# Two cross-attention blocks on one core: layer 1 keys and values from one column-tiled product, keys copied through DRAM, strided 32x32 transposes, all orders rewritten

## The reference

```python
# layer 0
qn, kn, vn = ln(x), ln(ctx), ln(ctx)
p = softmax((qh @ kh.T + rel_bias[idx]) / 8)            # 16 heads, 128 x 128 each
x = x + (p @ vh) @ fc_w.T + fc_b
x = x + gelu(ln2(x) @ W1.T + b1) @ W2.T + b2
# layer 1
q = x @ Wq + bq                                         # 16 heads of 16
k = ctx @ Wk + bk;  v = ctx @ Wv + bv                   # one head of 16 each
attn = softmax(window(q @ k.T / 4)) @ v @ Wo + bo
gate = silu(concat(attn, x) @ Wg + bg)
out = attn * gate + x * (1 - gate)
y = out * rsqrt(mean(out * out) + 1e-6) * rms_w
return y - mean(y over tokens)
```

## Time and profile before

| what | value |
|---|---|
| runs | 1901.46, 1903.86, 1906.15 us, median 1903.86 |
| profiled execution: its own time, and its span from first to last instruction | on record only as the span, 1903.7 us on its one core |
| PE busy | 1840.5 us, 97% |
| PEld, DVE, ACT, POOL busy | 89%, 80%, 81%, 68% |
| the chain that ended last | PE 94%, DMA 2%, DVE 1%, ACT 1%, POOL 1%, issue 1% |
| DMA | 214.49 MB, 113 GB/s mean |

### The profile page before, as it was taken

How to read it: one execution, slowest core, us unless ns; L and a number is a source line. 1 busy time by engine, 2 the same in 40 slices (tenths; PEclk the granted TensorE clock), 3 DMA queues, 4 the chain that set the end, 5 groups by cost and what they waited for, 6 DMA issues and landing times.

```text
span 1903.7 us, 55010 instructions
## 1 busy us (share of the span) xinstructions
PE 1840.5 (97%) x18660; PEld 1696.0 (89%) x18660; DVE 1518.9 (80%) x6787; ACT 1538.4 (81%) x5586; POOL 1294.2 (68%) x1328
## 2 busy tenths in 40 slices
PE   5999999999999999999999999999999999999974
PEld 4899999999999999999999999999999999999963
DVE  6768888888888888888888888888888888878764
ACT  4688888888888888888888888888888888888864
POOL 3547776767776767777766777766777776777654
PEclk9999999999999999999999999999999999999997
DMA  6434444444444444454434454444444444444332
GB/s 208 131 84 116 111 119 111 115 110 115 107 118 120 115 107 114 104 123 121 116 99 121 101 125 118 114 102 118 111 118 118 110 107 113 112 116 114 88 83 56
DMA packets 215273, 214.49 MB, mean 113 GB/s; under 512 B 29904, under 2 KB 197456, under 8 KB 214992
## 3 DMA queue, kind: packets, MB, share of 16 engines
q1 hardware_dynamic: 214992, 210.97, 44.5%
HBM read 67.23 MB, written 9.44 MB: 40 GB/s over the span
## 4 chain that ended last, share of the span: by engine, by line
PE 94%; DMA 2%; DVE 1%; ACT 1%; POOL 1%; issue 1%; SPq 0%; ACTq 0%; DVEq 0%; POOLq 0%
PE bank L576 12%; PE bank L577 11%; PE bank L578 11%; PE bank L594 8%; PE bank L590 8%; PE bank L591 8%; PE bank L757 7%; PE bank L770 7%; PE bank L582 4%; PE bank L882 4%; PE bank L895 3%; PE bank L583 3%; PE bank L586 3%; PE bank L654 2%; PE bank L600 2%
## 5 line engine op out<-in xcount | busy, mean ns | idle before, releaser
L2574 ACT ACTIVATE soft<-soft,row_min 128x128 f32<-128x128 f32 x1024 | 397.4, 393 | 16.3 <-DVE row_min L1728 16.0
L2494 ACT ACTIVATE soft<-soft,row_min 128x128 f32<-128x128 f32 x1024 | 397.8, 394 | 9.5 <-DVE row_min L1620 9.1
L235 DVE STREAM_TRANSPOSE turned<-soft 128x512 f32<-128x512 f32 x512 | 349.2, 692 | 9.7 <-POOL soft L3032 4.9
L3032 POOL TENSOR_TENSOR soft<-soft,inv_sum 128x512 f32<-128x512 f32 x256 | 267.1, 1044 | 127.3 <-DVE inv_sum L1628 123.3
L3041 POOL TENSOR_TENSOR soft<-soft,inv_sum 128x512 f32<-128x512 f32 x256 | 264.9, 1045 | 93.0 <-DVE inv_sum L1737 93.0
L1620 DVE CUSTOM_DVE_ANT_0 soft<-bank,relb 128x128 f32<-128x128 f32 x1024 | 231.6, 284 | 64.9 <-PE bank L757 64.5
L1728 DVE CUSTOM_DVE_ANT_0 soft<-bank,winb 128x128 f32<-128x128 f32 x1024 | 226.6, 284 | 16.9 <-PE bank L882 14.5
L2494 ACT ACTIVATION_READ_ACCUMULATOR soft<-soft,row_min 128x1 f32 x1024 | 196.7, 192 | 0.0
L2574 ACT ACTIVATION_READ_ACCUMULATOR soft<-soft,row_min 128x1 f32 x1024 | 195.1, 191 | 0.0
L1691 DVE TENSOR_TENSOR hidS<-hid,hidS 128x1024 fp32r<-128x1024 f32 x64 | 120.5, 1883 | 71.5 <-ACT hidS L2545 68.6
L757 PE MATMUL bank<-kT,qT 64*128 64x128 f32 x2048 | 148.7, 285 | 1.5 <-DVE kT L1600 1.4
(11 more groups left out here) (255 smaller groups left out, 6538.3 us busy)
## 6 DMA issues: line engine op xcount, KB each, us to landing
soft<-turned SPq DMA_DIRECT2D x1024, 128.0 KB, 2.8
tokens<-stats_by_row SPq DMA_DIRECT2D x63, 256.0 KB, 3.3
tokens<-in_x SPq DMA_DIRECT2D x32, 256.0 KB, 3.1
raw<-in_x_t SPq DMA_DIRECT2D x32, 256.0 KB, 2.8
x<-in_x SPq DMA_DIRECT2D x32, 256.0 KB, 3.1
out<-gate SPq DMA_DIRECT2D x63, 128.0 KB, 3.1
tokens<-in_ctx SPq DMA_DIRECT2D x31, 256.0 KB, 2.8
raw<-in_ctx_t SPq DMA_DIRECT2D x31, 256.0 KB, 2.8
```

Source lines behind the costliest of these rows:

```text
L235: return eng.transpose(turned[:, slot, :, s % 2, :, :].rearrange("p j h b -> p h j b"), soft[:, s, :, :].rearrange("p h (j a) -> p h j a", ...
L2494: last = act.activation(soft[:, s, h, :], soft[:, s, h, :], ACT.Exp, bias=row_min[:, s, h:h + 1], scale=-1.0, accum_out=row_sum[:, s, h:h ...
L2574: last = act.activation(soft[:, s, h, :], soft[:, s, h, :], ACT.Exp, bias=row_min[:, s, h:h + 1], scale=-1.0, accum_out=row_sum[:, s, h:h ...
L3032: pool.tensor_tensor(soft[:, m % NS0, :, :], soft[:, m % NS0, :, :], inv_sum[:, m % NS0, :].unsqueeze(2).broadcast_to([P, QUAD, SEQ]), ALU ...
```

## The change

One product `kv` takes the place of `kv_k` and `kv_v`: `Wk` and `Wv` side by side (32 columns), in column quarters, in block order. It gives each quarter of a bank 16 rows of keys and 16 rows of values for 32 tokens of each batch. `kv_turn` adds the key bias while it copies the whole piece (128x64) to `key_rows`, and transposes the same piece to `by_key`; `kv_out` puts the values once into the middle of `vpad`. The keys go to DRAM by four DMAs (`keys_out`) and back by two (`keys_in`) to the even rows of `kpar[:, 0]` and the odd rows of `kpar[:, 1]`; the other rows are zeros written once. The columns of `Wq` of layer 1 are mixed in pairs to fit. The keys now stand in token order: `k_out` reads the bank without a step, and `turn_blocks` reads every fourth element of a row instead. The constants `block_of`, `pair_of` and `parity` go. `scores1` waits for `keys_in`, not `kv_out`. The rings of banks and the lists of all five engines are written anew.

```diff
-        wkv1 = sb("wkv1", [P, KD, P + 2 * HD])
+        wkv1 = sb("wkv1", [P, KD, 2 * HD])
...
         def turn_blocks(eng, slot, s):
             return eng.transpose(turned[:, slot, :, s % 2, :, :].rearrange("p j h b -> p h j b"),
-                                 soft[:, s, :, :].rearrange("p h (j a) -> p h j a", j=NB))
+                                 soft[:, s, :, :].rearrange("p h (a j) -> p h j a", j=NB))
...
+            def keys_out(g):
+                if not there(g):
+                    return
+                till.wait_ge("kv_turn", g + 1)
+                if g >= 1:
+                    till.wait_ge("keys_in", 32 * g)
+                for j in range(NB):
+                    sp.dma_start(t["key_rows"][:, :, j, :], key_rows[j * BLOCK:j * BLOCK + HD, :, :]).then_inc(
+                        sem["keys_out"], 16)
+
+            def keys_in(g):
...
+                    till.wait_ge("scores1", GROUP * g)
+                till.wait_ge("keys_out", 16 * NB * (g + 1))
+                rows_of = t["key_rows"].rearrange("e b j a -> e (b j a)").unsqueeze(0).broadcast_to([NT1, HD, TOK])
+                for i in range(2):
+                    sp.dma_start(kpar[i:P:2, i, :], rows_of).then_inc(sem["keys_in"], 16)
...
-                for k in range(KD):
-                    last = pe.matmul(bank[:, 0:TOK], wkv1[:, k, 0:P], src[:, k, :], start=(k == 0), stop=(k == KD - 1))
-                last.then_inc(sem["kv_k"], 1)
...
-                        last = pe.matmul(bank[j * BLOCK:(j + 1) * BLOCK, TOK:TOK + GROUP * BLOCK], wkv1[:, k, P:P + HP],
+                        last = pe.matmul(bank[j * BLOCK:(j + 1) * BLOCK, 0:GROUP * BLOCK], wkv1[:, k, :],
                                          of_block[:, j, :, :], start=(k == 0), stop=(k == KD - 1), skip_group_check=True)
-                last.then_inc(sem["kv_v"], 1)
+                last.then_inc(sem["kv"], 1)
...
-                for i in range(2):
-                    dve.tensor_scalar(kpar[:, i, :].rearrange("p (b j a) -> p b j a", b=GROUP, j=NB),
-                                      bank[:, 0:TOK].rearrange("p (b a j) -> p b j a", b=GROUP, j=NB), bk1[:, 0:1],
-                                      parity[:, i:i + 1], ALU.add, ALU.mult)
-                dve.transpose(v_twice[:].rearrange("p b e -> p (b e)"), bank[:, TOK:TOK + GROUP * BLOCK]).then_inc(
-                    sem["kv_turn"], 1)
+                of_bank = bank[:, 0:GROUP * BLOCK]
+                dve.tensor_scalar(key_rows[:].rearrange("p b a -> p (b a)"), of_bank, bk1[:, 0:1], None, ALU.add)
+                dve.transpose(by_key[:].rearrange("p b e -> p (b e)"), of_bank).then_inc(sem["kv_turn"], 1)
...
-                    last = dve.tensor_scalar(kT[:, c, :].rearrange("p (b j a) -> p b j a", b=GROUP, j=NB),
-                                             bank[:, c * TOK:(c + 1) * TOK].rearrange("p (b a j) -> p b j a", b=GROUP, j=NB),
-                                             bk[:, i:i + 1], None, ALU.add)
+                    last = dve.tensor_scalar(kT[:, c, :], bank[:, c * TOK:(c + 1) * TOK], bk[:, i:i + 1], None, ALU.add)
```

Of the rewritten order of DVE's prologue:

```diff
             moments_x(0)
+            var_x(0)
             stats_c(0)
             moments_c(0)
-            bias_out(bq, banks[5], 2, -SCALE0)
-            var_x(0)
+            flip_x(0)
+            var_c(0)
...
```

More of the change, by code:

```diff
@@ L19 @@
 PER_GROUP = dict(
-    turn_h=1, turn_x2=1, kv_k=1, kv_v=1, proj_q=4, proj_k=4, proj_v=4, scores=4, turn0=8, pv=4,
+    turn_h=1, turn_x2=1, kv=1, proj_q=4, proj_k=4, proj_v=4, scores=4, turn0=8, pv=4,
     fc=4, fc_lo=4, w1=4, w2=4, w2_lo=4, out_mm_lo=2, q1=1, scores1=2, turn1=8, pv1=4, out_mm=2, center=2,
@@ L640, in wo_wg, with kv @@
                 last.then_inc(sem["wo_wg"], 1)
-            def kv_k(g, bank, *drains):
+            def kv(g, bank, *drains):
                 if not there(g):
@@ new lines, in tensor_program @@
+            proj_q(0, 0, banks[7])
+            kv(0, banks[6])
+            bias_mm(banks[5], SOFT1, 1, shifts[2], 0)
+            bias_mm(banks[5], SOFT0, 2, shifts[2], 1)
+            proj_q_lo(0, banks[7])
+            proj_k(0, 0, banks[0], ("bias", 1))
+            proj_k_lo(0, banks[0])
+            proj_k(0, 1, banks[3], ("bias", 2))
+            proj_q(0, 1, banks[1])
+            scores(0, 0, (banks[7], banks[4]), (("q_out", 1),), ())
+            proj_v(0, 0, banks[0], ("k_out", 1))
@@ new lines, in tensor_program @@
+            scores(0, 1, (banks[1], banks[5]), (("q_out", 2),), (("bias", 3),))
+            bias_mm(banks[7], SOFTT1, 2, shifts[3], 0, ("min0", 1))
+            proj_v(0, 1, banks[2])
+            proj_k(0, 2, banks[6], ("kv_turn", 1))
+            proj_v(0, 2, banks[4], ("min0", 2))
+            proj_q(0, 2, banks[1], ("min0", 3))
+            proj_q(0, 3, banks[3], ("k_out", 2))
+            proj_k(0, 3, banks[1], ("q_out", 3))
+            scores(0, 2, (banks[5], banks[6]), (("min0", 4),), (("k_out", 3),))
@@ new lines, in tensor_program @@
+            bias_mm(banks[7], SOFT1, 2, shifts[3], 1)
+            pv(0, 0, banks[0], ("v_out", 1))
+            fold_bv(banks[3], ("q_out", 4))
+            wo_wg(banks[2], 0, ("v_out", 2))
+            proj_q(1, 0, banks[3], ("bias", 4))
+            wo_wg(banks[2], 1)
+            proj_q_lo(1, banks[3])
+            pv(0, 1, banks[6], ("min0", 6))
+            scores(0, 3, (banks[0], banks[5]), (("o_lo", 1),), (("min0", 5),))
+            kv(1, banks[1], ("k_out", 4))
+            fc(0, 0, banks[7], ("bias", 5))
@@ new lines, in tensor_program @@
+            pv1(0, 0, 0, banks[1], ("x1", 2))
+            proj_k(2, 2, banks[7], ("k_out", 10))
+            scores(2, 1, (banks[0], banks[6]), (("min1", 5),), (("o_lo", 8),))
+            pv1(0, 0, 1, banks[1])
+            proj_q(2, 2, banks[3], ("min1", 6))
+            turn_h(1, banks[0], ("min0", 19))
+            out_mm(0, 0, banks[7], ("k_out", 11))
+            mlp_in(1, 0, banks[1], ("o1_lo", 1))
+            mlp_in_lo(1, banks[1])
+            scores(2, 2, (banks[3], banks[6]), (("q_out", 11),), (("min0", 20),))
@@ L2116, in vector_program @@
+            stats2_(NG - 4)
             turn0(NG - 3, 1)
[L2117 to L2130 removed]
```

2494 lines of the change are left out of this document (1220 added, 1274 removed).

## The result

| | before | changed |
|---|---|---|
| median of the runs | 1904.05 us (4 runs) | 1932.94 us (4 runs, 1927.15 to 1935.70) |
| ratio, with its 95% interval | | 1.0147 (1.0129 to 1.0165) |
| profiled span | 1903.7 us | 1931.9 us |
| a round, mean of 22 in the middle | 56.75 us | 57.87 us |

What follows compares the result with a forecast made beforehand. PE's list of work was taken to bound each round. From 1903.7 us, 27.8 (product), 16.3 (edges) and 7 (start) came off and 4 (allowance) was added: 1856.6, so 1857 us, 2.5% faster, range 1844 to 1872.

Steps and rivals of the forecast that it cites:

- The step that failed: DVE in the loop: strided SBUF reads add 0.15 us to each of 16 transposes, 2.4 us a round, at no price.
- The cover: DVE's idle time in a round: 47.6 us of work in some 55 leaves 7 us idle, so slower transposes cost nothing.
- Rival (b): Strided transposes make DVE the bound: 0.53 us more each, deciding from 0.4 us, rounds of 58.8 us, time 1946; 9%.
- The product (27.8 us): PE, the full product kv_k that goes: 0.87 us a group, 27.8 us less over 32 groups.
- the edges (16.3): PE, changes between full and packed products: 86 fewer at 0.19 us, three a round, 16.3 us less.
- Rival (a): Only the product goes: edges are paid between packed steps too and the start gains nothing; 1876 us, 12%.
- The wait that moves (0.17): PE: the 0.17 us wait of scores1 for q1T goes, another arises between scores of quarters 0 and 1; they cancel.
- DVE without the strides: DVE's work per round before the strided reads are added: 0.8 us less from kpar writes, 0.6 less from k_out.
- SP and the copy (0): SP: six more issues a round, 3.6 us, and a key copy of 9.2 us, with over 80 us of room; price 0.
- The start (7): Before the loop: earlier variance, statistics transpose and raw loads bring the first projection forward; gain 7 us, between 0 and 10.
- End and allowance: Last softmaxes and chain: 0, between -4 and +4; looser new orders on five engines: 0.15 us a round, 4 us lost.

## Why the prediction was wrong, and where it was right

**The step that failed** is "DVE. Added: 16 transposes ... 0.15 us for 512, 2.4 us a round ... the cover stays (7 us idle), and the price is 0". Two things in it were wrong.

The size: 0.41 us instead of 0.15, within the bounds of 0 to 0.53 but near the upper one. This was the smaller fault: with 0.41 the same comparison gives 45.2 + 6.6 = 51.8 us of DVE's work in a round of 55.45, still below it, and again a price of 0. Measured, the 16 strided reads cost 2.5 us a round (57.87 against 55.37) and 82 us in all. I took the value from `k_out` as the nearest row. That row had a strided read of PSUM, and its 74 ns over another instruction were not the price of the step at all: in step it takes 469 to 472 ns as well. A row of the other memory was no neighbour. The rule of the Trainium skill that I set against it (Advanced Engine Details and Errata, SBUF Cachelines) was right for SBUF.

The cover: I compared DVE's sum with the round. Rival (b) did the same, with a threshold of 0.4 us. Its 1946 came within 13 us of the result, but by luck: with the measured 0.41 in place of its 0.53 its rule gives a round of 45.2 + 6.6 + 5.05 = 56.85 and some 1895 us, and its reason is not what the runs show. DVE stays idle for 6.7 of 57.9 us (1158.10 busy of 1310 us). Eight strided reads cost 7 us of the time in layer 0 and 49 in layer 1. What counts is how far DVE has come in its list when the input of a step arrives that PE or ACT waits for: two transposes right ahead of `k_out`, six in the unbroken stretch ahead of `hid_lo`, four ahead of `x_hat` and so of ACT's values.

**The product (27.8 us)** and **the edges (16.3)**: right in their sum, but hidden by the transposes. Product and three edges should take 0.87 + 0.57 = 1.44 off a round; the version with contiguous transposes has 56.74 - 55.33 = 1.41 less. No run takes the edges alone, so how the 1.41 is shared is not shown. (That each of the packed steps had full products before and behind it in the old kernel is not exact, as the earlier trace rows has two of them together. But counted in the traces, with transposes as packed work, the entries from full products are 298 and 213, so 85 fewer.) Between packed products its timeline shows no price: scores hold PE for 1.09 ahead of `pv`, `pv` 1.02 ahead of `turn_h` and of `pv1`, `scores1` 1.08 ahead of `pv`. Rival (a) is out. That the product is worth its length held only with the new orders; alone in the old ones it brought 4 us. "A microsecond off that list is one off each round as long as nobody becomes late" was the right sentence, and in the old orders somebody becomes late at once.

**The wait that moves (0.17)**: right. Where `pv` stands between the scores of quarters 0 and 1, it holds PE for 1.22 instead of 1.03, and 0.19 is the wait:

```profile
946.53 1.16 PE L777 MATMUL bank<-kT,qT 64*128 64x128 f32 x16
947.62 0.55 PE L790 MATMUL bank<-soft,V 128*64 128x128 f32 x6
...
948.84 1.16 PE L777 MATMUL bank<-kT,qT 64*128 64x128 f32 x16
```

**DVE without the strides**: I had 46.6 - 0.8 - 0.6 = 45.2 us a round. It is 45.8 (1085.38 / 1310 x 55.33): the 0.8 came, the 0.6 of `k_out` did not.

**SP and the copy (0)**: right in the new orders, where PE never waits for keys. In the old ones it cost some 5 us.

**The start (7)**: 8.7 us in the change (19.33 against 28.04). **End and allowance**: the spans 1903.7 and 1850.1 differ by 53.6 us. Up to the first `scores1` of group 1 it is 8.3, no more than the start; over the 26 rounds from there it is 37.2, and behind them 8.1. How much of the 8.1 is product and edges and how much the end itself, the runs don't separate. The allowance of 4 was not needed.

Without the strided reads the time is 1850.7, within 0.4% of the sum of 1857. So one term, put at nothing, decided the sign.

## What to carry to other kernels

Idle time of an engine is no cover for a slower instruction until one has looked, at each step that others wait for, how long the engine has worked without a gap ahead of it, and how many of the slower instructions stand in that stretch. Moving such a step ahead of its input blocks what is behind it; whether a smaller move would have helped was not tried. And where one part of a change has a price that no row shows, run it alone: here one line hid a gain of 52 us.

## What the runs showed of the hardware

- A DVE read of fp32 from SBUF with a step of 4 elements or more costs 0.36 us more for 512 elements (675 to 1037 ns; 0.41 in this kernel), at a step of 3 some 0.15, at 2 nothing. For `tensor_scalar` it is 0.19 (481 to 668), and a write with a step of 4 costs as much as the read (transposes 1057, `tensor_scalar` 661).
- A read of PSUM by `tensor_scalar` takes the same at steps of 1 and 4 (477 and 477 ns for 256 elements).
- Packed steps of different kinds follow each other on PE at no price: scores (row halves) hold it for 1.09 us whether `pv` (column halves) or a full product follows, and `pv` then holds it for 1.02, as it does behind a full product. `scores1` holds it for 1.08 ahead of `pv` and of `pv1`.
- A full product of four matmuls between two packed ones lengthened a round by 1.20 us, where a product of that shape between scores and a full product was worth 0.86. Why was not tried.
